# Expert stages of a two-layer block: where the key scores are copied, when their exponentials run, and in which order the dot products and expert products are issued

## The reference, cut to what matters

```python
x = x + 0.5 * _L0_ffn_ref(_layernorm(x), ...)     # expert stage f1
x = x + _L0_attn_ref(_layernorm(x), ...)
x = x + 0.5 * _L0_ffn_ref(_layernorm(x), ...)     # expert stage f2, the same code
x = x + 0.5 * _L1_ffn_ref(_layernorm(x), ...)
x = x + _L1_attn_ref(_layernorm(x), ...)
x = x + 0.5 * _L1_ffn_ref(_layernorm(x), ...)

def _L0_ffn_ref(hidden_states, W_up, W_down, W_q, keys, down_embed, up_embed):
    q = einsum('btd,ed->bte', hidden_states, W_q)            # two halves x 4 heads
    sim = einsum('pbthn,hkpn->pbthk', q, keys)               # 2 x 4 x 64 key scores a row
    (sx, sy), (ix, iy) = top_k(sim, 8)
    all_scores = sx[..., :, None] + sy[..., None, :]         # 64 candidates a head
    scores, pk = top_k(all_scores, 8)
    de, ue = down_embed[indices], up_embed[indices]          # 1024 experts
    w = silu(einsum('btd,bthkd->bthk', hidden_states, de) * softmax(scores))
    experts_states = einsum('bthk,bthkd->btd', w, ue)
    dense = einsum('bti,di->btd', silu(einsum('btd,id->bti', hidden_states, W_up)), W_down)
    return dense + experts_states
```

## Time and profile before

| | before |
|---|---|
| median of three runs | 4204.2 us (4195.04 to 4204.57) |
| profiled execution, its time | 4200.71 us |
| its span in the profile | 4197.8 us |
| stage f1, 32 turns | about 0 to 1200 us of the span |
| stage f2, 32 turns | about 2294 to 3500 us |
| TensorE, VectorE, ScalarE, GpSimd busy | 89%, 78%, 62%, 58% of the span |

### The profile page before, as it was taken

One profiled execution on the slowest core, in us unless ns is written; L12 is line 12 of the kernel. 1 busy time (PEld: TensorE's weight loads), 2 busy tenths in 40 slices (PEclk: granted clock), 3 DMA queues, 4 the chain that ended last, 5 costly groups with the idle time before them and its releaser, 6 DMA issues. The chain is left out here.

```text
span 4197.8 us, 79094 instructions
## 1 busy us (share of the span) xinstructions
PE 3733.1 (89%) x27416; PEld 3195.1 (76%) x27416; DVE 3256.6 (78%) x7738; ACT 2618.8 (62%) x7750; POOL 2451.0 (58%) x2330
## 2 busy tenths in 40 slices
PE   6888888888869999999997788888888887999989
PEld 5777777777757888888886677777777776988878
DVE  7888888888748888888875788888888875866577
ACT  4555555555539999999995555555555545733156
POOL 6666666666635555546541767666666654711266
PEclk9999999999989999999998999999999998999999
DMA  4554555555520000000001355555545553331342
GB/s 113 105 103 100 101 101 104 104 103 106 101 74 7 22 22 12 22 17 17 22 7 53 86 106 106 102 105 101 105 99 101 100 99 94 121 109 54 126 144 96
DMA packets 190350, 343.11 MB, mean 82 GB/s; under 512 B 14817, under 2 KB 138113, under 8 KB 189953
## 3 DMA queue, kind: packets, MB, share of 16 engines
q0 software_dynamic: 55296, 201.35, 25.3%
q1 hardware_dynamic: 134656, 136.71, 10.3%
HBM read 80.06 MB, written 56.62 MB: 33 GB/s over the span
## 5 line engine op out<-in xcount | busy, mean ns | idle before, releaser
L300 POOL TENSOR_TENSOR f_grid<-f_ex 128x1024 f32<-128x1024 f32 x512 | 1075.5, 2153 | 289.6 <-DVE f_q L692 289.5
L683 DVE SCALAR_TENSOR_TENSOR f_p_u<-f_grid,f_te,f_p_dot 128x1024 f32<-128x1024 f32 x512 | 653.2, 1276 | 175.0 <-PE f_p_dot L106 174.4
L1514 ACT ACTIVATE a_ex<-a_p_s,a_mneg 128x128 f32<-128x128 f32 x2048 | 725.9, 406 | 90.3 <-DVE a_mneg L1568 90.3
L692 DVE SCALAR_TENSOR_TENSOR f_q<-f_p_u,f_rz,f_grid 128x1024 f32<-128x1024 f32 x512 | 652.1, 1274 | 4.8
L310 POOL DMA_DIRECT2D f_q<-f_q x384 | 398.4, 1038 | 431.3 <-DMA f_q<-f_q 290.3
L445 PE MATMUL f_p_y<-f_wdn,f_hs 128*128 128x256 f32 x2048 | 469.7, 382 | 45.0 <-ACT f_hs L547 44.0
L1514 ACT ACTIVATION_READ_ACCUMULATOR a_ex<-a_p_s,a_mneg 128x1 f32 x2048 | 502.4, 245 | 0.0
L450 PE MATMUL f_p_y<-f_eup,f_wT 128*128 128x256 f32 x2048 | 476.0, 381 | 0.0
L445 PEld LDWEIGHTS f_p_y<-f_wdn,f_hs 128*128 128x128 f32 x2048 | 383.3, 190 | 110.6 <-ACT f_hs L547 57.0
L533 ACT ACTIVATE f_ex<-f_p_sim,f_negm 128x64 f32<-128x64 f32 x1024 | 223.5, 329 | 341.4 <-PE f_p_sim L106 298.0
L450 PEld LDWEIGHTS f_p_y<-f_eup,f_wT 128*128 128x128 f32 x2048 | 385.8, 191 | 55.2
(11 more groups left out here) (644 smaller groups left out, 11099.0 us busy)
## 6 DMA issues: line engine op xcount, KB each, us to landing
f_q<-f_q POOLq DMA_DIRECT2D x384, 512.0 KB, 4.8
x_f<-f_yt SPq DMA_DIRECT2D x64, 256.0 KB, 4.0
f_xt<-x SPq DMA_DIRECT2D x32, 256.0 KB, 4.3
a_xt<-x_f SPq DMA_DIRECT2D x16, 512.0 KB, 3.8
x_a<-a_yt SPq DMA_DIRECT2D x16, 512.0 KB, 2.9
f_xt<-x_a SPq DMA_DIRECT2D x32, 256.0 KB, 4.3
c_xt<-x_f SPq DMA_DIRECT2D x16, 512.0 KB, 4.7
x_c<-c_yt SPq DMA_DIRECT2D x16, 512.0 KB, 3.2
```

What stands on the lines that cost most here:

```text
L300: g_grid.mark(pool.tensor_tensor(grid[v][:, hd, :].rearrange("p (i j) -> p i j", i=XROWS), sx[:, hd, :].unsqueeze(2).to_broadcast([P, XROW ...
L683: d_mask.mark(dve.scalar_tensor_tensor(out=p_u[:], in0=grid[v][:, hd, :], scalar=te[:, v, hd, TOP - 1:TOP], in1=p_dot[:], op0=ALU.is_ge, o ...
L692: d_mul.mark(dve.scalar_tensor_tensor(out=q[v][:, hd, :], in0=p_u[:], scalar=rz[:, v, hd:hd + 1], in1=grid[v][:, hd, :], op0=ALU.mult, op1 ...
L1514: last = act.activation(ex[t.step % 2][:, i, n, :], p_s[i][:, n, :], ACT.Exp, bias=mneg[:, i, n:n + 1], accum_out=z[t.step % 2][:, i, n:n ...
```

## The change

The key scores get an SBUF buffer `sim`. ScalarE copies each block's scores from `p_sim` (new function `similar` and track `a_sim`), VectorE's `lowest` and ScalarE's `exps` read the copy, and TensorE waits for the copy instead of the exponentials before it writes `p_sim` again. Both blocks' scores of turn t + 2 are now made and copied in the middle of turn t, and both blocks' exponentials stand together at the turn's end. TensorE issues `dots(t + 1, 0)` right behind the first transpose, and the second transpose and both expert products of block 0 go to the next turn. `turn_w(t - 1, 1, 1)` and `experts(t - 1, 1, 0)` go behind `dots(t, 1)`. The tail term is added to head 3 and not to head 2, behind `back`; `summed` waits accordingly. VectorE's `output` goes from behind head 0 to behind head 1, and GpSimd issues `tails` ahead of the last add.

```diff
-        ex = m.sbuf("ex", V, 2 * HEADS * KEYS)
+        sim, ex = (m.sbuf(k, V, 2 * HEADS * KEYS) for k in ("sim", "ex"))
...
                 def summed(t, v, k):
 
-                    a_silu.wait(pool, t, (f"front{v}", f"clamped{v}", f"back{v}")[k])
+                    a_silu.wait(pool, t, (f"front{v}", f"third{v}", f"clamped{v}")[k])
                     if k:
                         s_add[v][k - 1].wait(pool, t)
                     s_add[v][k].mark(pool.dma_start(q[v][:, 0, :], q[v][:, k + 1, :], accum_op=ALU.add))
...
                 def step(t):
                     after = (t + 1).exists(last=count)
+                    tails(t, 0)
                     if (t - 1).exists():
                         summed(t - 1, 1, 2)
-                    tails(t, 0)
                     if after:
                         scores(t + 1, 0, (0, 1))
                     summed(t, 0, 0)
...
                 def turn_h(t):
                     a_h.wait(pe, t)
                     if (t - 1).exists():
-                        a_ex.wait(pe, t - 1, "1")
+                        a_sim.wait(pe, t - 1, "1")
...
@@ -390,7 +390,7 @@
                         a_hT.wait(pe, t)
                         d_hT.wait(pe, t)
                     else:
-                        a_ex.wait(pe, t, "0")
+                        a_sim.wait(pe, t, "0")
...
                 def step(t):
                     before, after, later = (t - 1).exists(), (t + 1).exists(last=count), (t + 2).exists(last=count)
+                    if before:
+                        turn_w(t - 1, 0, 1)
                     hidden(t, 0)
-                    if after:
-                        similar(t + 1, 1)
+                    if before:
+                        experts(t - 1, 0, 0)
+                        experts(t - 1, 0, 1)
+                    hidden(t, 1)
                     if before:
                         dense(t - 1, 1)
                         turn_w(t - 1, 1, 0)
-                    hidden(t, 1)
-                    if before:
-                        turn_w(t - 1, 1, 1)
-                        experts(t - 1, 1, 0)
                     if later:
                         turn_h(t + 2)
                     dots(t, 1)
                     if before:
+                        turn_w(t - 1, 1, 1)
+                        experts(t - 1, 1, 0)
                         experts(t - 1, 1, 1)
+                    if later:
+                        similar(t + 2, 0)
                     hidden(t, 2)
+                    if later:
+                        similar(t + 2, 1)
                     hidden(t, 3)
                     dense(t, 0)
                     turn_w(t, 0, 0)
-                    if later:
-                        similar(t + 2, 0)
-                    turn_w(t, 0, 1)
                     if after:
                         dots(t + 1, 0)
-                    experts(t, 0, 0)
-                    experts(t, 0, 1)
                 turns(pe, count, unroll, step)
...
+                def similar(t, v):
+                    t_sim.wait(act, t, str(v))
+                    a_sim.mark(act.copy(sim[:, v, :], p_sim[:]), str(v))
+
                 def exps(t, v):
 
-                    t_sim.wait(act, t, str(v))
                     d_neg.wait(act, t, str(v))
                     if (t - 1).exists():
                         g_grid.wait(act, t - 1, f"{v}3")
                         d_top.wait(act, t - 1, f"maxes{v}")
                     for n in range(2 * HEADS):
-                        last = act.activation(ex[:, v, n * KEYS:(n + 1) * KEYS], p_sim[:, n * KEYS:(n + 1) * KEYS],
+                        last = act.activation(ex[:, v, n * KEYS:(n + 1) * KEYS], sim[:, v, n * KEYS:(n + 1) * KEYS],
                                               ACT.Exp, bias=negm[:, v, n:n + 1])
                     a_ex.mark(last, str(v))
...
 
                     d_mul.wait(act, t, f"{v}2")
                     a_silu.mark(act.activation(q[v][:, 2, :], q[v][:, 2, :], ACT.Silu), f"third{v}")
+
+                def back(t, v):
+
+                    d_mul.wait(act, t, f"{v}3")
+                    a_silu.mark(act.activation(q[v][:, 3, :], q[v][:, 3, :], ACT.Silu), f"back{v}")
                     g_tail.wait(act, t, f"use{v}")
                     a_silu.mark(act.activation(w8[:, v], u8[:, v], ACT.Silu, accum_out=clamped[:, v:v + 1]), f"tail{v}")
                     a_silu.wait(act, t, f"tail{v}")
-                    a_silu.mark(act.activation(q[v][:, 2, EXPERTS - 1:EXPERTS], q[v][:, 2, EXPERTS - 1:EXPERTS],
+                    a_silu.mark(act.activation(q[v][:, 3, EXPERTS - 1:EXPERTS], q[v][:, 3, EXPERTS - 1:EXPERTS],
                                                ACT.Identity, bias=clamped[:, v:v + 1]), f"clamped{v}")
-
-                def back(t, v):
-
-                    d_mul.wait(act, t, f"{v}3")
-                    a_silu.mark(act.activation(q[v][:, 3, :], q[v][:, 3, :], ACT.Silu), f"back{v}")
...
                 def step(t):
-                    before, after, later = (t - 1).exists(), (t + 1).exists(last=count), (t + 2).exists(last=count)
+                    before, later = (t - 1).exists(), (t + 2).exists(last=count)
+                    if before:
+                        turned(t - 1, 0, 1)
                     if later:
                         normed(t + 2)
-                    if after:
-                        exps(t + 1, 1)
                     hidden(t, 0)
+                    front(t, 0)
+                    hidden(t, 1)
+                    third(t, 0)
                     if before:
                         turned(t - 1, 1, 0)
-                    front(t, 0)
-                    hidden(t, 1)
-                    if before:
-                        turned(t - 1, 1, 1)
-                    third(t, 0)
                     back(t, 0)
                     if later:
                         turn_h(t + 2)
+                    if before:
+                        turned(t - 1, 1, 1)
+                    if later:
+                        similar(t + 2, 0)
+                    front(t, 1)
                     hidden(t, 2)
+                    if later:
+                        similar(t + 2, 1)
+                    third(t, 1)
                     hidden(t, 3)
-                    front(t, 1)
-                    third(t, 1)
+                    back(t, 1)
                     turned(t, 0, 0)
-                    back(t, 1)
-                    turned(t, 0, 1)
                     if later:
                         exps(t + 2, 0)
+                        exps(t + 2, 1)
                 turns(act, count, unroll, step)
...
                 def lowest(t, v):
 
-                    t_sim.wait(dve, t, str(v))
-                    d_neg.mark(dve.tensor_reduce(negm[:, v, :], p_sim[:].rearrange("p (n k) -> p n k", k=KEYS), AX.X,
+                    a_sim.wait(dve, t, str(v))
+                    d_neg.mark(dve.tensor_reduce(negm[:, v, :], sim[:, v, :].rearrange("p (n k) -> p n k", k=KEYS), AX.X,
                                                  ALU.max, negate=True), str(v))
...
                 def step(t):
                     before, after, later = (t - 1).exists(), (t + 1).exists(last=count), (t + 2).exists(last=count)
                     for v in range(V):
                         mask(t, v, 0)
                         weigh(t, v, 0)
-                        if before:
-                            output(t - 1, v)
-                        if v == 0 and after:
-                            lowest(t + 1, 1)
-                        if v == 1 and later:
+                        if v and later:
                             turned(t + 2)
                         if after:
                             maxes(t + 1, v, range(0, 3))
@@ -756,9 +771,13 @@
                         if after:
                             maxes(t + 1, v, range(3, 5))
                         weigh(t, v, 1)
+                        if before:
+                            output(t - 1, v)
                         if after:
                             maxes(t + 1, v, range(5, 8))
                         mask(t, v, 2)
+                        if v and later:
+                            lowest(t + 2, 0)
                         if after:
                             maxes(t + 1, v, range(8, 10))
                         weigh(t, v, 2)
@@ -770,10 +789,10 @@
                         if after:
                             best(t + 1, v)
                             inverse(t + 1, v)
+                    if later:
+                        lowest(t + 2, 1)
                     if (t + 3).exists(last=count):
                         front(t + 3)
-                    if later:
-                        lowest(t + 2, 0)
                 turns(dve, count, unroll, step)
```

More of the change, by code:

```diff
@@ L221, in expert_ffn @@
         t_sim = m.track("t_sim", "0", "1")
-        d_neg = m.track("d_neg", "0", "1")
+        a_sim, d_neg = m.track("a_sim", "0", "1"), m.track("d_neg", "0", "1")
         a_ex = m.track("a_ex", "0", "1")
```

(53 more changed lines are left out.)

## The result

The changed kernel takes 4071.8 us, the median of four runs (4069.9 to 4075.8), against 4204.4 before (four runs, 4195.0 to 4208.2). The ratio is 0.9689, 95% interval 0.9671 to 0.9707. The forecast was 4079. The profiled execution's span is 4068.1 us where it was 4197.8.

What follows compares the result with a forecast made beforehand. No engine was full; a circle of waits of 35.86 us a turn bound the kernel. The new turn, 33.33 + 0.53 = 33.86, saves 125.6 us over two stages, giving 4075, plus 3.5 for the median: 4079 us, range 4017 to 4139.

Steps and rivals of the forecast that it cites:

- The circle: Longest loop of waits across the engines in one new turn: 33.33 us, or 33.86 with the exponentials' SBUF cost.
- three pieces: First transpose to silu 0, 8.74 us; silu 0 to mask 1, 9.48; mask 1 to first transpose, 15.11.
- The exponentials from SBUF: ScalarE's 16 exponentials a turn, reading SBUF instead of PSUM, cost 0.53 us more, bounds nothing to 1.06.
- my term: 33 ns extra for each of 16 exponentials from SBUF, 0.53 us a turn, from two 128x512 activation rows.
- the slower rival: ScalarE's 16 exponentials lose their overlap, 0.36 us or more each; at 0.42 the time is 4249 us; chance 0.09.
- lower bound: No extra cost for exponentials from SBUF, if the surplus lies in the overlap of neighbours.
- TensorE's waits: TensorE waits 1.4 us before hidden 1, some 0.7 for hidden 3 and 1.5 for dense 0.
- The DMA adds: Adds feeding block 1's transpose have some 3 us slack; block 0's are in by 26, its transpose at 30.
- The opening and the end: Per stage: two copies before the first turn lose 1.2 us; the end after the last masks changes nothing, within 2.

Runs made afterwards that it cites:

- the padding runs: Changed kernel with four extra ScalarE copies a turn: behind both blocks' exponentials 4146.1 us, ahead of the copy of block 0's key scores 4068.2 us.
- the gains that add: Changed kernel with silus of hidden 2 and 3 ahead of front and third: 4000.2 us; with normalisation behind hidden 1's silu: 4015.4; with both: 3942.2.
- two runs with the expert order alone: Kernel before with early dots, block 0's experts next turn, no key-score copies: 4519.7 us; same with block 0's key scores kept ahead of dots: 4257.2 us.

## Why the prediction was right

- *The circle.* Right, and each of its three pieces within 0.03 us. VectorE's list from mask 1 to the product of head 2 was 8.64 us and not 8.74, and dense 0 3.55 and not 3.46. That it sets the time is shown by the padding runs and by the gains that add.
- *The exponentials from SBUF.* The sum took 0.53 us, the two 128x512 rows' difference for each of 16. Measured: 517.78 - 513.94 = 3.84 us for 16 where they took 3.16, so 0.68 more, 43 ns each, though the 16 also stand in one row now where they stood in two. "VectorE: DVE Perf Modes" of the Trainium skill, in the section on the TRN2 errata, gives a difference of 52 cycles, the 0.69 us stated in the prediction as an estimate; the trace agrees with it better than my term. What hid this was that the copy of the second transpose took 0.47 to the next start and not 0.58, and `normed` 1.10 and not 1.14.
- *The overlap of the exponentials (the slower rival).* Wrong here: 0.24 us from start to start at a duration of 0.33. The prediction's lower bound put the surplus into the overlap, and in the trace it is the overlap that shrinks: the mean duration of one is 329 ns from PSUM and 334 from SBUF.
- *TensorE's waits.* At the right places, but 2.74 us in all and not 3.6. The wait ahead of hidden 1 is 0.5 short, and part of it lies earlier: the weight load of block 0's second half of experts waits some 0.4 us for the second copy, which the prediction did not place.
- *The DMA adds.* Right that they have slack in the new order. The third add of block 1 waits 2.48 us for the second, and in the turns nothing on TensorE waits for a DMA. In two runs with the expert order alone TensorE did wait for the adds, 3.3 us and 2.3, and both are slower than the kernel before; those runs keep the old list of ScalarE.
- *The opening and the end.* Mis-sized on both sides. The opening cost 4.5 us in each stage and not 1.2; the prediction priced the two copies and left out the collision of VectorE and GpSimd and VectorE's waits for both maxima. The end of f1 gained, where I said nothing: from the mask of turn 31 to the start of the next stage's first load it was 1199.7 - 1148.6 = 51.1 us and is 1133.1 - 1087.6 = 45.5. `front` of block 0 goes ahead of a copy that waits for TensorE, and the chain of adds starts 7.5 us behind the mask and not 11.4.
- *Luck in the total.* By the masks f1 gains 66.6 us (58.67 in the turns, 6.86 in the last one, 5.6 at the end, less 4.5 in the opening) and f2 64.8 (63.3, 3.2 and 2.8, less 4.5), where the forecast had 62.8 for each, and the last part of the program takes 1.7 more; that is 129.7 of the span. The turn was right by its working. That the sum came within 7 us also took errors that cancel, and the last turns and ends hang on the clock that each got.
- *Not foreseen.* That the expert order needs the other parts. I expected most of the gain of this order alone, and it loses 39 to 316 us, while the other parts without it gain 76.

## What to carry to other kernels

Where no engine is full, write down the circle of waits with start-to-start times of the trace and price an edit as what it adds and takes on that circle; the same work off it costs nothing. When a piece is moved, follow every engine's list behind it to the next wait, since an early issue can hold up what another engine reads first. And when TensorE's waits grow, look at the granted clock: behind such a wait its own work was slower, and a loss of 3 us a turn became one of 5.4. A mean clock hides this: turns of one kernel differed by 1.3 to 1.6 us with the clock that each got.

## What the runs showed of the hardware

Two VectorE instructions of 128x1024 with both inputs in SBUF took 5.61 us instead of 2.34 when GpSimd had started its grids 0.23 us ahead of them, and the four grids took 9.45 instead of 7.49. In the kernel before, the VectorE pair started first, 0.17 us ahead of GpSimd's candidates (128x512); it took 2.34 and the candidates 3.10, where they took 1.06 at 31.58 us. The second stage repeats both cases within 0.02 us. The masks and products, with one input in PSUM, stay at 1.27 us beside grids of 1.90. Small exponentials cost 43 ns more from SBUF than from PSUM by the distance of their starts, and only 5 ns more by their duration. Behind waits of TensorE of 2.17, 3.3 and 4.4 us the granted clock had stretches at 1.2 GHz (products of 0.63 us that take 0.40 at 2.4 GHz). Behind the wait of 2.2 us this happened in four of five turns. The wait of 4.4 us was followed in turn by a shorter and a longer such stretch (dense 0 5.24 and 6.59 us, 3.55 at the full clock). No wait of the changed kernel's turns, of at most 1.29 us, had one.
